# Gathering the softmax numerators of each head on ScalarE instead of VectorE (preln attention and RWKV feed-forward, 8 cores)

## The reference, cut to what matters

```python
strain = disp_win - disp[:, :, :, None, :]
bond_act = gelu(strain @ W_strain + rel_emb @ W_pos)
bond_logits = (bond_act @ W_bond)[..., 0]
damage = sigmoid((gelu(strain @ W_dmg + b_dmg) @ W_dmg_out)[..., 0] + b_dmg_out[0])
weights = softmax(where(cmask, bond_logits - 10.0 * damage, -inf), axis=-1)   # over 64 places
out = einsum('bntd,bntde->bnte', weights, val_win)
x = x + out.reshape(B, T, C) @ W_cproj
```

## Time and profile before

| | us |
|---|---|
| median of 2 runs | 3227.46 (3227.26 to 3227.66) |
| the profiled execution, own time | 3229.14 |
| its span on the slowest core (core 5) | 3227.6 |
| spans of the 8 cores | 3219.8 to 3227.6 |

### The profile page before, as it was taken

How to read it: one execution, slowest core, us unless ns; L and a number is a source line. 1 busy time by engine, 2 the same in 40 slices (tenths; PEclk the granted TensorE clock), 3 DMA queues, 4 the chain that set the end, 5 groups by cost and what they waited for, 6 DMA issues and landing times.

```text
span 3227.6 us, 21862 instructions; the slowest of 8 cores (3219.8 to 3227.6 us)
## 1 busy us (share of the span) xinstructions
PE 1695.5 (53%) x4568; PEld 471.2 (15%) x4568; DVE 831.3 (26%) x2474; ACT 1101.4 (34%) x1500; POOL 17.3 (1%) x32
## 2 busy tenths in 40 slices
PE   0055545535554445435555545554555466767776
PEld 0011111101111111111111112211212111111111
DVE  0012223253223433342222231111223242232101
ACT  0014556446554555724434423333111010111010
POOL 0000000000000000000000000000000000000000
PEclk9999555556565556656556555555555555555555
DMA  8400000010000100031101011011121101001001
GB/s 129 104 27 10 10 10 20 4 20 10 14 7 13 20 10 10 4 62 30 33 27 27 26 39 36 27 33 36 40 62 56 39 13 46 33 20 39 29 23 46
DMA packets 134678, 100.43 MB, mean 31 GB/s; under 512 B 111120, under 2 KB 112288, under 8 KB 134560
## 3 DMA queue, kind: packets, MB, share of 16 engines
q1 hardware_dynamic: 125152, 78.88, 9.1%
q0 software_dynamic: 9408, 20.15, 3.2%
HBM read 74.86 MB, written 35.40 MB: 34 GB/s over the span
## 4 chain that ended last, share of the span: by engine, by line
PE 42%; ACT 24%; issue 20%; DVE 8%; DMA 5%; DVEq 0%; ACTq 0%; SPq 0%
ACT s_actT L443 11%; ACT s_actT L433 7%; PE ps L695 5%; PE ps L927 5%; PE ps L899 5%; PE ps L873 5%; PE ps L283 5%; DMA Ebuf<-s_zero 4%; PE ps L456 4%; PE ps L619 2%; PE ps L615 2%; DVE s_eh L497 2%; PE ps L304 2%; PE ps L644 2%; PE ps L638 2%
## 5 line engine op out<-in xcount | busy, mean ns | idle before, releaser
L456 PE MATMUL ps<-s_actT,s_bd 128*32 128x512 bf16 (+1 forms) x1280 | 463.7, 510 | 623.4 <-ACT s_actT L443 452.7
L443 ACT ACTIVATE s_actT<-s_argT,s_pcols 128x512 bf16<-128x512 bf16 (+1 forms) x640 | 369.4, 648 | 43.3 <-DVE s_argT L422 31.0
L422 DVE TENSOR_TENSOR s_argT<-s_dD 128x512 bf16<-128x512 bf16 (+1 forms) x640 | 203.7, 381 | 395.6 <-ACT s_actT L433 232.7
L433 ACT ACTIVATE s_actT<-s_argT,s_bdmgc 128x2048 bf16<-128x2048 bf16 x128 | 256.5, 2004 | 61.7 <-DVE s_argT L422 50.5
L456 PEld LDWEIGHTS ps<-s_actT,s_bd 128*32 128x32 bf16 x1280 | 126.3, 120 | 935.6 <-issue 922.5
L422 DVE TENSOR_TENSOR s_argT<-s_dS 128x512 bf16<-128x512 bf16 (+1 forms) x640 | 203.5, 381 | 223.6 <-ACT s_actT L443 159.4
L927 PE MATMUL ps<-s_wval,s_kact 128*128 128x512 bf16 x256 | 149.5, 584 | 60.2 <-DVE s_x2r L936 23.8
L873 PE MATMUL ps<-s_xk,s_wkT 128*128 128x512 bf16 x256 | 149.5, 584 | 58.4 <-DVE s_xk L859 20.3
L695 PE MATMUL ps<-s_wcp,s_atok 128*128 128x512 bf16 x272 | 152.2, 560 | 49.5 <-ACT s_atok L668 10.0
L283 PE MATMUL ps<-s_wval,s_lnfm 128*128 128x512 bf16 x272 | 145.6, 535 | 49.0 <-ACT s_lnfm L272 9.3
L899 PE MATMUL ps<-s_wrT,s_xr 128*128 128x512 bf16 x256 | 149.5, 584 | 38.2
(11 more groups left out here) (110 smaller groups left out, 1298.1 us busy)
## 6 DMA issues: line engine op xcount, KB each, us to landing
s_wbt<-Ebuf SPq DMA_DIRECT2D x68, 191.0 KB, 3.3
Ebuf<-s_zero SPq DMA_DIRECT2D x16, 544.0 KB
X2buf<-s_xrel SPq DMA_DIRECT2D x17, 512.0 KB, 2.6
s_x<-X2buf POOLq DMA_DIRECT2D x17, 512.0 KB, 4.0
s_xt<-xs SPq DMA_DIRECT2D x33, 256.0 KB, 3.9
s_xrel<-xs SPq DMA_DIRECT2D x33, 256.0 KB, 4.1
s_x2r<-X2buf SPq DMA_DIRECT2D x16, 512.0 KB, 3.7
out<-s_x2r SPq DMA_DIRECT2D x16, 512.0 KB, 2.6
```

The source lines that it names most:

```text
L422: (lambda e: e.tensor_sub(s_arg[slot][:, 0:W], srcT[:, srcOff + c0 - 63 + j: srcOff + c0 - 63 + j + W], srcT[:, srcOff + c0: srcOff + c0 + ...
L433: P.emit("scalar", (lambda half=half: (lambda e: e.activation(out=s_actT[:, 2048 * half:2048 * half + 2048], in_=s_argT[:, 2048 * half:204 ...
L443: P.emit("scalar", (lambda slot=slot, W=W, bias=bias: (lambda e: e.activation(out=s_act[slot][:, 0:W], in_=s_arg[slot][:, 0:W], func=AF.Ge ...
L456: (lambda e: e.matmul(PS[bank][32 * q:32 * q + 32, 0:W], s_bd32[:, pi * 128 + v * 32: pi * 128 + v * 32 + 32], s_act[slot][:, 0:W], start= ...
```

## The change

The 16 gathers with their sums leave VectorE: each `tensor_scalar` (times 1.0, accumulated by add) becomes an `activation` with the function Copy and an accumulator output on ScalarE. The copy L484 and the reciprocal L502 stay on VectorE. The semaphores follow: the reciprocal waits for ScalarE ("ss"), the copy of block ts waits until ScalarE has read the single `s_etok` of block ts - 1 (`css`), the first gather of a chunk waits for the DMAs that still read `s_eh` on ScalarE's queue instead of VectorE's, and the first DMA of `s_eh` waits for the last gather instead of the last reciprocal. Nothing else is touched; lines behind L475 have numbers one higher in the changed kernel, and those behind L504 two higher.

```diff
@@ -472,6 +472,7 @@
         compact_ts = {}
+        css = {}
         for ts in range(nts):
...
             P.emit("vector", (lambda ts=ts, bank=bank: (lambda e: e.tensor_copy(
                 s_etok[ts % 2][:, :], PSB[bank][:, 0:1024])))(),
-                waits={"st": P.now("st")}, inc="sv")
+                waits={"st": P.now("st"), "ss": css.get(ts - 1, 0)}, inc="sv")
...
-                P.emit("vector", (lambda srcap=srcap, hG=hG, ts=ts, zc=zc: (lambda e: e.tensor_scalar(
-                    out=s_eh[:, hG * 256 + ts * 64: hG * 256 + ts * 64 + 64], in0=srcap,
-                    scalar1=1.0, scalar2=None, op0=ALU.mult, op1=ALU.add,
-                    accum_out=s_zsum[:, zc:zc + 1])))(),
-                    waits=wvv if hG == 0 else None, inc="sv")
+                P.emit("scalar", (lambda srcap=srcap, hG=hG, ts=ts, zc=zc: (lambda e: e.activation(
+                    out=s_eh[:, hG * 256 + ts * 64: hG * 256 + ts * 64 + 64], in_=srcap,
+                    func=AF.Copy, accum_out=s_zsum[:, zc:zc + 1])))(),
+                    waits=wvv if hG == 0 else None, inc="ss")
+            css[ts] = P.now("ss")
             P.emit("vector", (lambda gtb=gtb: (lambda e: e.reciprocal(
                 s_zrec[:, (gtb - 1) * 16:(gtb - 1) * 16 + 16], s_zsum[:, (gtb - 1) * 16:(gtb - 1) * 16 + 16])))(),
-                inc="sv")
+                waits={"ss": css[ts]}, inc="sv")
             compact_ts[ts] = P.now("sv")
         compact_done[ci] = P.now("sv")
+        cd_ss = P.now("ss")
...
-                   waits={"sv": compact_done[ci], "dz": dz_all} if hG == 0 else None,
+                   waits={"ss": cd_ss, "dz": dz_all} if hG == 0 else None,
```

## The result

The changed kernel took 3260.18 us (median of 7 runs, 3258.44 to 3262.14) against 3228.53 us (6 runs) of the kernel before on the same chip: a ratio of 1.0099 with a 95% interval of 1.0087 to 1.0111. It is 31.7 us slower, where 15.5 us were forecast. The time lies in the range that was given, and within 2%, but the cost is a little over twice the one forecast. The profiled execution took 3260.9 us, its span on the slowest core is 3259.4 us, and the granted clock is that of before (0.585 in the mean).

A forecast was written before the change was run, and what follows sets the result against it. The prediction took 16 serial gather blocks at the ends of chunks 0 to 3 to bound the kernel. With chunk 4, 272 s - 104.2 us at s = 0.44 gave 3227.5 + 15.5 = 3243 us, range 3220 to 3280.

The forecast's parts named there:

- What bounds the kernel: Gather blocks at chunk ends: 16 of 17 serial on the path, the one at chunk 4 hidden beside other work.
- The formula of the time in s: Added time over all blocks, s being ScalarE's step per gather: 272 s - 104.2 us, +15.5 us at s = 0.44.
- The duration of a gather: A ScalarE Copy of 64 elements from SBUF: 258 ns, from rows of 1 and 512 neighbouring fp32 elements.
- The accumulator read and its overlap: After each ScalarE gather, as in the layer norm: step is the duration plus 0.18 us, read 0.19 us.
- The changes of engine: Per block: VectorE to ScalarE 0.15 us, first gather 0.84 us after the copy's start; ScalarE to VectorE 0.17 us.
- Chunk 4: Gathers now stand ahead of ScalarE's copies of `pa1`, delaying TensorE's third group of transposes: 2.7 us more.
- Activation tables: ScalarE at chunk ends: no new table load expected; one at each end would be 6 us.
- rival 1: ScalarE gathers: the stride costs twice the per-element time, s = 0.494, +30 us, 3258 us; chance 0.20.
- the 42 ns of VectorE: VectorE's 264 ns gather against 222 ns by its rows of neighbouring elements: 42 ns longer, by pattern or by kind.
- Rivals 2, 3 and 4: Accumulator read hides, 3218 us, 0.12; nothing overlaps in short instructions, 3291 us, 0.05; blocks not on path, 3230 us, 0.05.

The follow-up runs named there:

- the shared version: The changed kernel, but heads 8 to 15 gathered on VectorE again beside heads 0 to 7 on ScalarE: 3195.03 us, ratio 0.9892 to the kernel before.

## Why the prediction was wrong in size and right in kind

- **What bounds the kernel:** right. 16 blocks serial, one beside other work; the shared version moved the time by the expected amount (35 us for 36).
- **The formula of the time in s:** right. 272 s - 104.2 gives +31.8 us at the measured s = 0.50, and +15.5 at 0.44; the measured differences of the changed kernel and of the one with neighbouring elements are 31.7 and 16.3 us. That 31.8 meets 31.7 so closely is partly luck. The prediction took the first block's 7.52 us for all 16, whose mean was 7.64; the formula has 16 x (9.28 - 7.52) = 28.2 us for them where 27.2 were measured, 3.7 for chunk 4 where it was 4.1, and 0.5 us have no place.
- **The duration of a gather:** this is the step that failed. "Duration of a Copy of 64 elements from SBUF", 258 ns, was worked out from rows that read neighbouring elements, and the prediction said so in the same breath, but took it as the value. For neighbouring elements it was right (257 ns); with this kernel's 16 bytes between elements it measured 315 ns, and 272 x 0.057 = 15.5 us of the 16.2 us that the forecast lacked are this. "I take 0.44, since the layer norm's rows have the very pair of instructions" rested on the kind of instruction and left out its pattern.
- **The accumulator read and its overlap:** right. 188 ns, beginning 0.22 us after the start of a gather of 0.315, so 0.095 before its end, and the step is the duration plus 0.185 (0.18 forecast).
- **The changes of engine:** right in the usual block (0.15 us after the copy's end, 1927.48 - 1926.64 = 0.84). In some blocks, such as the first of chunk 0, it was 0.43 us; why was not tried. In chunks 1 to 3 the first block of the kernel before had such a step too (0.40 us), and the chunk ends grow by 6.5 to 7.3 us where 4 x (9.28 - 7.52) = 7.0 was due.
- **Chunk 4:** right in place. The formula gives 16 x 0.50 - 4.33 = 3.7 us at the measured step, and 4.1 us were lost. The copy begins 2323.69 - 2323.32 = 0.37 us behind the next block's first transpose where it was 0.03; the first gather follows the copy's end by 0.38 us instead of 0.15; and from the copy to s_wb to the transpose it is 0.25 us and not the 0.39 that was taken. Together that is the 0.4 us. This was read from the traces only; no run kept chunk 4 alone on VectorE.
- **Activation tables:** as forecast, no new loads: 36 at the gelu of L443 and 31 at the exp in both kernels.
- **The rivals:** rival 1 was the case: s = 0.494 and +30 us were worked out, at a chance of 0.20. The prediction had its evidence in hand, the 42 ns of VectorE at this very pattern, and argued it down by "VectorE paid less than its own per-element time". The experiments show that VectorE's excess was the stride's own (44 ns), so the better reading was that ScalarE would pay at least the like, and that alone would have given 3243 + 272 x 0.042 = 3254 us. Rivals 2, 3 and 4 did not happen.

## What to carry to other kernels

Moving work from one engine to another pays only if something runs beside it; where the steps wait for each other, compare the two engines' steps (duration, accumulator read, wait), not their busy shares. A duration may be taken from another row only if the access pattern is the same too. And 16 small instructions in a line are first to be tried as one with a pattern of more dimensions: here a copy and a reduction in their place won 49 us on the same engine, and 69 us with the bank read directly, where sharing the gathers between engines won 35 and moving them lost 32.

## What the runs showed of the hardware

- A ScalarE Copy of 64 bf16 elements from SBUF took 257 ns for neighbouring elements, 259 at 8 bytes apart, 287 at 12, 315 at 16 and 316 at 32 (12 and 32: one run each). VectorE's gather with accumulator took 220 and 264 ns for neighbouring elements and at 16 bytes.
- At 16 bytes apart, 1024 bf16 elements in one VectorE reduction took 1948 to 1953 ns from SBUF and 1225 ns from PSUM. A reduction of 1024 neighbouring fp32 elements from SBUF took 1220 ns. So the stride cost the reduction 0.71 ns per element in SBUF and nothing in PSUM.
- The same elements in one VectorE copy took 1065 ns from SBUF and 1225 ns from PSUM, where the copy of 1024 neighbouring elements from PSUM took 692 ns. So the copy's pattern cost 533 ns from PSUM. The strided copies also write in another order, and no run has a plain copy from SBUF; what each part costs there was not tried.
- Gathers of ScalarE and VectorE on one SBUF tile at the same time kept their durations (315 and 265 ns).
